# Two-layer gated expert network with a dense tower: order of the first transfers and of the first unit's products

## The reference

```python
e = jnp.stack([tbl_0[ids[:, 0]], ..., tbl_4[ids[:, 4]]], axis=1)     # 1024 rows x 5 tables x 1024
def _ple_layer(x, W, b, Gw, Gb, Gsw=None, Gsb=None):                 # 10 experts: 2 per task (4 tasks), 2 shared
    xe = x[:, EXPERT_IN_IDX, :]
    eo = jax.nn.relu(jnp.einsum('bed,edh->beh', xe, W) + b)          # each 1024 x 1024
    gates = jax.nn.softmax(jnp.einsum('btd,tdk->btk', x[:, :T, :], Gw) + Gb, axis=-1)
    task_out = jnp.einsum('btk,btkh->bth', gates, eo[:, SEL, :])
    if Gsw is None:
        return task_out
    gs = jax.nn.softmax(x[:, T, :] @ Gsw + Gsb, axis=-1)
    shared_out = jnp.einsum('be,beh->bh', gs, eo)
    return jnp.concatenate([task_out, shared_out[:, None, :]], axis=1)
z = _ple_layer(_ple_layer(e, W0, b0, G0w, G0b, Gs0w, Gs0b), W1, b1, G1w, G1b)
h = jnp.concatenate([z.reshape(1024, -1), dense_ctx], axis=1)
h = jnp.maximum(h @ W_top1 + b_top1, 0.0)
h = jnp.maximum(h @ W_top2 + b_top2, 0.0)
y = h @ W_top3
```

## Time and profile before

| | us |
|---|---|
| median of 3 runs | 1983.0 (1982.62 to 1983.07) |
| profiled execution, its own time | 1983.02 |
| its span | 1981.0 |
| TensorE busy | 1973.8 |
| VectorE busy | 1352.5 |
| ACT busy | 702.6 |
| GpSimd busy | 170.1 |

### The profile page before, as it was taken

How to read it: one execution, slowest core, us unless ns; L and a number is a source line. 1 busy time by engine, 2 the same in 40 slices (tenths; PEclk the granted TensorE clock), 3 DMA queues, 4 the chain that set the end, 5 groups by cost and what they waited for, 6 DMA issues and landing times.

```text
span 1981.0 us, 25278 instructions
## 1 busy us (share of the span) xinstructions
PE 1973.8 (100%) x8898; PEld 1612.3 (81%) x8898; DVE 1352.5 (68%) x1335; ACT 702.6 (35%) x934; POOL 170.1 (9%) x152
## 2 busy tenths in 40 slices
PE   9999999999999999999999999999999999999999
PEld 7878878888788888888878788788887888888887
DVE  6488988895256765667555888898943666556564
ACT  3333233333233233332434233323333333433333
POOL 5630000000030002122033000000000000000000
PEclk9999999999999999999999999999999999999999
DMA  7543434333253334344344434334332424333331
GB/s 228 171 156 109 131 95 130 128 96 100 85 164 96 117 96 149 106 147 121 96 144 135 133 94 130 103 116 136 96 100 76 124 92 127 97 116 96 117 96 43
DMA packets 69102, 232.24 MB, mean 117 GB/s; under 512 B 10037, under 2 KB 11325, under 8 KB 69033
## 3 DMA queue, kind: packets, MB, share of 16 engines
q1 hardware_dynamic: 60664, 210.30, 34.6%
q0 software_dynamic: 7488, 20.98, 3.3%
q10 hardware_dynamic: 880, 0.10, 0.0%
HBM read 230.27 MB, written 1.08 MB: 117 GB/s over the span
## 4 chain that ended last, share of the span: by engine, by line
PE 99%; DMA 0%; ACT 0%; issue 0%; POOL 0%
PE main L370 30%; PE main L371 29%; PE main L372 29%; PE top L371 3%; PE top L370 3%; PE top L372 3%; PE gps L423 1%; PE gps L435 1%; DMA eo_sh<-in_tbl,idx 0%; PE gps L410 0%; PE top L503 0%; DMA idx<-in_ids 0%; ACT eo_b L795 0%; PE top L561 0%; PE main L561 0%
## 5 line engine op out<-in xcount | busy, mean ns | idle before, releaser
L370 PE MATMUL main<-act_hi,w_hi 128*128 128x512 f32 (+1 forms) x2576 | 1002.0, 389 | 0.0
L371 PE MATMUL main<-act_lo,w_hi 128*128 128x512 f32 (+1 forms) x2576 | 1000.5, 388 | 0.0
L372 PE MATMUL main<-act_hi,w_lo 128*128 128x512 f32 (+1 forms) x2576 | 1000.5, 388 | 0.0
L932 DVE TENSOR_TENSOR w_lo<-raw,w_hi 128x1024 fp32r<-128x1024 f32 (+1 forms) x356 | 433.7, 1218 | 587.2 <-ACT w_hi L626 563.8
L626 ACT ACTIVATE w_hi<-raw 128x1024 fp32r<-128x1024 f32 (+1 forms) x356 | 376.4, 1057 | 1219.5 <-PE main L372 1109.1
L370 PEld LDWEIGHTS main<-act_hi,w_hi 128*128 128x128 f32 x2576 | 483.6, 188 | 107.6 <-issue 6.4
L372 PEld LDWEIGHTS main<-act_hi,w_lo 128*128 128x128 f32 x2576 | 483.6, 188 | 100.2
L371 PEld LDWEIGHTS main<-act_lo,w_hi 128*128 128x128 f32 x2576 | 483.6, 188 | 99.0
L1051 DVE TENSOR_TENSOR slots<-slots,prod 128x1024 f32<-128x1024 f32 (+2 forms) x202 | 245.0, 1213 | 6.0
L361 POOL DMA_INDIRECT slots<-in_tbl,idx x144 | 166.0, 1153 | 894.5 <-DVE act_lo L944 605.8
L1045 DVE TENSOR_TENSOR prod<-eo_sh,gate_b 128x1024 f32<-128x1024 f32 x136 | 165.7, 1219 | 1.7
(11 more groups left out here) (78 smaller groups left out, 419.9 us busy)
## 6 DMA issues: line engine op xcount, KB each, us to landing
raw<-in_w SPq DMA_DIRECT2D x304, 512.0 KB
gate_b<-tasks_dram SPq DMA_DIRECT2D x32, 512.0 KB, 5.9
raw<-in_w_top SPq DMA_DIRECT2D x32, 512.0 KB
raw<-in_w_first SPq DMA_DIRECT2D x16, 512.0 KB
gate_b<-tasks_dram SPq DMA_DIRECT2D x16, 256.0 KB, 6.4
slots<-in_tbl,idx POOLq DMA_INDIRECT x144
gate_b<-gates_dram SPq DMA_DIRECT2D x2, 512.0 KB, 4.0
raw<-in_w_top SPq DMA_DIRECT2D x4, 256.0 KB
```

The costliest lines, as they stand in the source:

```text
L370: nc.tensor.matmul(dst, lhs_hi, rhs_hi, start=start, stop=False)
L371: nc.tensor.matmul(dst, lhs_hi, rhs_lo, start=False, stop=False)
L372: return nc.tensor.matmul(dst, lhs_lo, rhs_hi, start=False, stop=stop)
L932: nc.vector.tensor_tensor(w_lo[0:parts, slot, 0:cols], raw[0:parts, rawslot, 0:cols], w_hi[0:parts, slot, 0:cols], ALU.subtract).then_inc( ...
```

## The change

SP issues weight unit 0 first of all. The row numbers of the first four tiles (4 columns, 2 KB, a semaphore `idx0_in` of their own), the identity, the other row numbers, and all constants as one tensor `fixed` (190 columns) are issued by ACT. Units 1 and 2 are issued behind row tiles 2 and 3, then the gate weights, then unit 3. The warming is 13 matrix products of a zero tile (`blank`, cleared by VectorE as its first instruction) instead of 18 transposes of the identity, and starts before the identity is there. The first unit's products of the first columns are taken apart: the high x high products (`x0_main`) of strips 0 to 3 stand behind tile 1, those of strips 4 to 7 inside tile 2, the others (`x0_cross`) around the rest of tile 2 and tile 3. The second columns are as before. The first bank of the turned strips is `main[1]` in place of `main[0]`.

```diff
-WARM = 18
+WARM = 13
+FIXED = (NE * KT, NE * KT, MT1, MT2, MT2, GBIAS)
...
-        bias0 = sb("bias0", [P, NE * KT])
-        bias1 = sb("bias1", [P, NE * KT])
-        tower_c = sb("tower_c", [P, MT1 + 2 * MT2])
+        fixed = sb("fixed", [P, sum(FIXED)])
+        cuts = np.cumsum((0, *FIXED)).tolist()
+        bias0, bias1, bias_t1, bias_t2, w3, gbias = (fixed[:, a:b] for a, b in zip(cuts, cuts[1:]))
...
-        x0_bank = [main[0], gps[1]] + top + [gps[0], main[1]]
+        x0_bank = [main[1], gps[1]] + top + [gps[0], main[1]]
+        blank = eo_b[:, 0, 0:P]
...
-            sp.dma_start(idx[:, :], ids).then_inc(idx_in, 16)
-            sp.dma_start(ident, ident_in).then_inc(ident_rdy, 16)
-            sp.dma_start(gw[:, :, :].rearrange("p k n -> p (k n)"), gs_first).then_inc(gw_in, 16)
...
-                    for c in range(RAW):
-                        if c:
-                            sp.wait_ge(x0_in[c], 16)
-                        unit(w0_first, c, c, c)
+                    unit(w0_first, 0, 0, 0)
+                    sp.wait_ge(x0_in[NBT - 2], 16)
+                    unit(w0_first, 1, 1, 1)
+                    sp.wait_ge(x0_in[NBT - 1], 16)
+                    unit(w0_first, 2, 2, 2)
+                    sp.dma_start(gw[:, :, :].rearrange("p k n -> p (k n)"), gs_first).then_inc(gw_in, 16)
+                    unit(w0_first, 3, 3, 3)
...
-            pool.wait_ge(idx_in, 16)
+            pool.wait_ge(idx0_in, 16)
...
+            pe.wait_ge(blank_rdy, 1)
+            for n in range(WARM):
+                nc.tensor.matmul(gps[0][:, 0:P], blank, blank, start=True, stop=True)
             pe.wait_ge(ident_rdy, 16)
-            for n in range(WARM):
-                nc.tensor.transpose(gps[0][:, 0:P], ident, ident)
...
+            def x0_main(ks):
+                for k in ks:
+                    pe.wait_ge(act_hi_rdy, k // 2 + 1)
+                    nc.tensor.matmul(main[0][:, 0:X0_COLS], w_hi[:, 0, k * P:(k + 1) * P], act_hi[:, k, 0:X0_COLS],
+                                     start=(k == 0), stop=False)
+            def x0_cross(ks):
+                for k in ks:
+                    pe.wait_ge(act_lo_rdy, k // 2 + 1)
+                    w = slice(k * P, (k + 1) * P)
+                    nc.tensor.matmul(main[0][:, 0:X0_COLS], w_hi[:, 0, w], act_lo[:, k, 0:X0_COLS], start=False, stop=False)
+                    nc.tensor.matmul(main[0][:, 0:X0_COLS], w_lo[:, 0, w], act_hi[:, k, 0:X0_COLS],
+                                     start=False, stop=(k == KT - 1))
...
-            for bt in range(X0_HALF + 1):
-                x0_turn(bt)
+            x0_turn(0)
+            x0_turn(1)
             pe.wait_ge(hi_split, 1)
+            x0_main(range(4))
+            x0_turn(2, range(6))
+            x0_main(range(4, KT))
             pe.wait_ge(lo_split, 1)
-            x0_sums(0, range(2))
-            x0_turn(X0_HALF + 1)
-            x0_sums(0, range(2, KT))
-            x0_sums(1, range(KT)).then_inc(unit_done, 1)
+            x0_cross(range(2))
+            x0_turn(2, range(6, KT))
+            x0_cross(range(2, 4))
+            x0_turn(3)
+            x0_cross(range(4, KT))
...
-            for dst, src in ((bias0, b0), (bias1, b1), (bias_t1, b_top1), (bias_t2, b_top2), (w3, w_top3)):
-                act.dma_start(dst[:, :], src).then_inc(consts_in, 16)
-            act.dma_start(gbias[:, :], g_bias).then_inc(consts_in, 16)
+            act.dma_start(idx[:, 0:NBT], ids[:, 0:NBT]).then_inc(idx0_in, 16)
+            act.dma_start(ident, ident_in).then_inc(ident_rdy, 16)
+            act.dma_start(idx[:, NBT:], ids[:, NBT:]).then_inc(idx_in, 16)
+            act.dma_start(fixed[:, :], fixed_in).then_inc(consts_in, 16)
...
+            nc.vector.memset(blank, 0.0).then_inc(blank_rdy, 1)
             nc.vector.memset(turned[:, :, :], 0.0).then_inc(chain, 1)
```

More of the change, by code:

```diff
@@ L61, with build @@
 Q4 = 4
-WARM = 18
+WARM = 13
 ROWSETS = 5 * NBT
 GBIAS = NE + (T // DUO + 1) * T
+FIXED = (NE * KT, NE * KT, MT1, MT2, MT2, GBIAS)
 IDX = NBT + (ROWSETS * HALVES - NBT) * Q4
 RAW = 4
-def build(nc, ids, dense, tbl_0, tbl_1, tbl_2, tbl_3, tbl_4, w0_first, w0, w1, w_top, w_top2, w_top3,
-          b0, b1, b_top1, b_top2, gs_first, gs_w, g_w, g_bias, ident_in, out):
+def build(nc, ids, dense, tbl_0, tbl_1, tbl_2, tbl_3, tbl_4, w0_first, w0, w1, w_top, w_top2,
+          gs_first, gs_w, g_w, fixed_in, ident_in, out):
     f32, f32r, i32 = mybir.dt.float32, mybir.dt.float32r, mybir.dt.int32
@@ L101, in build @@
         turned = sb("turned", [DUO * GCOL, N // GCOL, GCOL])
-        gbias = sb("gbias", [P, GBIAS])
-        gbias_tasks = gbias[:, NE + T // DUO * NG:]
         blocks = N // GCOL
@@ L114, in build @@
         idx = sb("idx", [P, IDX], i32)
-        bias0 = sb("bias0", [P, NE * KT])
-        bias1 = sb("bias1", [P, NE * KT])
-        tower_c = sb("tower_c", [P, MT1 + 2 * MT2])
-        bias_t1, bias_t2, w3 = tower_c[:, 0:MT1], tower_c[:, MT1:MT1 + MT2], tower_c[:, MT1 + MT2:]
+        fixed = sb("fixed", [P, sum(FIXED)])
+        cuts = np.cumsum((0, *FIXED)).tolist()
+        bias0, bias1, bias_t1, bias_t2, w3, gbias = (fixed[:, a:b] for a, b in zip(cuts, cuts[1:]))
+        gbias_tasks = gbias[:, NE + T // DUO * NG:]
         gates_dram = nc.dram_tensor("gates_dram", (HALVES, GROWS * N), f32, kind="Internal").ap()
@@ L129, in build @@
         idx_in = sem("idx_in")
+        idx0_in = sem("idx0_in")
+        blank_rdy = sem("blank_rdy")
         raw_in = [sem(f"raw_in{i}") for i in range(RAW)]
@@ L548, in tower3, with x0_turn @@
                 mm.then_inc(y_done, 1)
+            pe.wait_ge(blank_rdy, 1)
+            for n in range(WARM):
+                nc.tensor.matmul(gps[0][:, 0:P], blank, blank, start=True, stop=True)
             pe.wait_ge(ident_rdy, 16)
-            for n in range(WARM):
-                nc.tensor.transpose(gps[0][:, 0:P], ident, ident)
-            def x0_turn(bt):
+            def x0_turn(bt, ks=range(KT)):
                 pe.wait_ge(x0_in[bt], 16)
                 half, c = divmod(bt, X0_HALF)
-                for k in range(KT):
+                for k in ks:
                     at = (k % 2) * X0_COLS + c * P
@@ L564, in x0_turn @@
                         mm.then_inc(x0_turned, 1)
-            def x0_sums(half, ks):
-                n = slice(half * X0_COLS, (half + 1) * X0_COLS)
+            def x0_main(ks):
                 for k in ks:
-                    pe.wait_ge(act_hi_rdy, half * (KT // 2) + k // 2 + 1)
-                    pe.wait_ge(act_lo_rdy, half * (KT // 2) + k // 2 + 1)
-                    w = slice(k * P, (k + 1) * P)
-                    mm = three(main[0][:, n], w_hi[:, 0, w], w_lo[:, 0, w], act_hi[:, k, n], act_lo[:, k, n],
-                               k == 0, k == KT - 1)
-                return mm
@@ L585, in _ @@
+            x0_cross(range(4, KT))
+            rest = slice(X0_COLS, N)
+            for k in range(KT):
+                pe.wait_ge(act_hi_rdy, KT // 2 + k // 2 + 1)
+                pe.wait_ge(act_lo_rdy, KT // 2 + k // 2 + 1)
+                w = slice(k * P, (k + 1) * P)
+                mm = three(main[0][:, rest], w_hi[:, 0, w], w_lo[:, 0, w], act_hi[:, k, rest], act_lo[:, k, rest],
+                           k == 0, k == KT - 1)
+            mm.then_inc(unit_done, 1)
             expert(1, 1, 1)
@@ L836, in _ @@
             split_hi(1, 1, 0)
-            act.wait_ge(consts_in, 16 * 6)
+            act.wait_ge(consts_in, 16)
             for h in range(HALVES):
@@ L1238, in _ @@
             x0_again(range(0, 2))
-            dve.wait_ge(consts_in, 16 * 6)
+            dve.wait_ge(consts_in, 16)
             turns = ({"A": {3: [(0, 0, 0)], 4: [(0, 0, 1)], 5: [(0, 0, 2)], 7: [(0, 0, 3)],
@@ L1378 @@
             a["W_top2"].reshape(2, 2, P, TOP2).transpose(0, 2, 1, 3).reshape(2, P, 2 * TOP2)),
-        "w_top3": per_part(a["W_top3"]),
-        "b0": per_part(a["L0_rec_b0"][order]), "b1": per_part(a["L0_rec_b1"][order]),
-        "b_top1": per_part(a["b_top1"]), "b_top2": per_part(a["b_top2"]),
         "gs_first": quad_cols(a["L0_rec_Gs0w"]),
@@ L1385 @@
                          for some in (*(_quarters(a["L0_rec_G0w"])[t:t + DUO] for t in range(0, T, DUO)), a["L0_rec_G1w"])]),
-        "g_bias": np.concatenate([
+        "fixed_in": np.concatenate([
+            per_part(a["L0_rec_b0"][order]), per_part(a["L0_rec_b1"][order]), per_part(a["b_top1"]), per_part(a["b_top2"]),
+            per_part(a["W_top3"]),
             np.tile(a["L0_rec_Gs0b"].reshape(1, -1), (P, 1)),
```

## The result

The changed kernel takes 1985.97 us in the median of 22 runs (1984.77 to 1987.24), the kernel before 1983.49 in 22 runs beside it (1982.52 to 1984.03): 2.5 us slower, ratio 1.0013 with a 95% interval of 1.0007 to 1.0018. It lies within 0.2% of before, but outside my range, which ended at 1985.4. The profiled execution is near the top of these, 1987.1 us of its own time, with a span of 1985.0 against 1981.0; its rows show more of the loss than the median has.

A forecast was written before the change was run, and what follows sets the result against it. TensorE, saturated after 12.6 us, bounds the kernel, so only the head can move. Tile 1's landing +0.4 (0.8 - 0.4) and order +0.4 give +0.8 us on 1983.02, shaded to +0.6: 1983.6 us, range 1981.6 to 1985.4.

The forecast's parts named there:

- Step (a): Row numbers on ACT's queue beside weight unit 0: they land 0.8 us later, bounds 0 and +1.4.
- Step (e): Warming by 13 zero products: ends before tile 0, costs nothing itself; clock taken to rise where it did.
- Rival 2: TensorE's clock rises 3 us later after the earlier end of warming: +1.5 us, 1985.1 us; chance 0.18.
- (b): Row tiles no longer meet weight unit 0 in the DMA queues: 0.4 us given back, bounds 0 and 0.9.
- (c): Later weights issued behind the row tiles still land in time: cost 0, without that cover up to 1 us.
- (d): ACT issues 4 transfers for 6, so unit 0's split may start at about 4.5 us: effect 0.
- (f): New product order: gaps behind tile 1 and a wait for VectorE before the logits, +0.4 us, bounds 0 and +0.9.
- Rival 1: Row numbers pass ahead of the weights and rows arrive up to 0.9 us earlier: -0.6, 1982.4 us; chance 0.22.
- Rival 4: ACT's transfers always reach the engines later than SP's; row numbers land with weight unit 0: +1.4, 1984.8 us; chance 0.09.
- the gather at 3.7 to 4.1 us: Sign for the row numbers' delay: GpSimd's first gather starts then instead of at 3.12 us.
- tile 1 at 10.4 to 11.0: Sign for the rows' landing: row tile 1 is there at 10.4 to 11.0 us.
- the turns of tile 0 at 0.23: Sign for the warming: turns of tile 0 and most of tile 1 spaced 0.23 us on TensorE.

The follow-up runs named there:

- e2: Changed kernel with 28 warming products instead of 13; 1984.69 us.
- e9: Kernel before with weight unit 0 first on SP, then identity and gate weights, and row numbers first on ACT; 1985.15 us.
- e1: Changed kernel with the first tiles' row numbers issued by SP ahead of weight unit 0; 1982.90 us.
- e5: Changed kernel with SP issuing weight unit 0 only once the row numbers on ACT's queue have landed; 1983.52 us.
- e7: Kernel before with 22 warming transposes instead of 18; 1983.06 us.
- e4: Changed kernel with row numbers on SP ahead of weight unit 0 and 20 warming products; 1982.57 us.
- e6: Kernel before with only the new warming, 13 products of a zero tile; 1983.04 us.
- e3: Changed kernel with the old order of the first unit's products and the old first bank; 1985.70 us.
- e10: e4 with units 1 to 3 issued behind row tiles 1 to 3 and gate weights behind unit 0, as before; 1982.84 us.
- e8: e4 with the old order of the first unit's products and the old first bank; 1982.87 us.
- e12: e4 repeated without change; 1982.76 us.

## Why the prediction was wrong

The bound was read rightly: nothing moved but the head, the logits' start moved by 3.93 us and the span by 4.0. The forecast's form (tile 1 later, less what the rows win) was right too, and the time still left its range, by two steps. The first alone would not have done it: e2, with the row numbers as late and the clock steady, has 1984.69 us, below the 1985.4 where the range ended.

**Step (a), mis-sized.** I put the row numbers' delay at +0.8 us, with +1.4 as the bound. It is +1.97 (4.81 against 2.84), and in e9 +1.7. The mechanism, packets taking turns with those of the weights, is what the queues show. The size failed in three terms. The row numbers' packets took 1.90 us from the first to the last start (2.34 to 4.24), not the 1.4 of 9 turns at 0.16, and 0.71 in the kernel before (1.75 to 2.46), so +1.2 for +0.8. The first of them started 0.6 us later than before, which I had put at nothing, and from the last to the landing it took 0.2 longer. The weight unit before was a guide at hand: issued at 2.13, split from 6.05, 3.9 us; "lands with the weights" meant at 0.75 + 3.9 = 4.65, so a bound of +1.8. The Trainium skill's sentence on round-robin by packets ("DMA: Bandwidth & Descriptors", Queues, rings and completion order) agrees with e1, e5 and e9 together in the direction; but by that page an engine drains a whole packet of typically 9 to 17 descriptors before it switches, which would be all of the 9 that it has of the weight unit, while here 70 of the row numbers' 128 pieces had started by 3.4 us. So they took turns in smaller portions. I had placed its result in my bounds, and should have taken it for the estimate.

**Step (e), "in the sum it rises where it did".** This was false. By the mean clock (0.998 or 0.999) in all 22 runs of the changed kernel it was low for a time after it had risen, for about 7 us in the profiled one. Rival 2 had the direction and the size (+1.5; e2 gives 1.3 in the median, and the profiled run ends unit 0 2.27 us later behind tile 1 than the one of before) but the wrong picture: not a rise that comes later, but a rise during the warming (28 products in e2 take 8.26 us, 0.29 each; the first 13 take 0.35 each) and a fall behind 3.95 us of idle time, the turns of tile 0 and 1.27 more. The fall is made by (a) and (e) together: warming ends at 5.6 instead of 7.3 us while tile 0 comes at 9.5 instead of 8.3. Shortening the pause from either side cures it: e1 (pause 1.70) in 8 of 11 runs, e2 (0.19) in all. That idle time is behind the fall is shown by this; how much of it is too much is not: 1.85 us let the clock stand in all runs of e7, 1.75 in 3 of 11 of e5, and e9 with 0.47 and then 1.50 in 7 of 11. I also took the one profiled run of before for the kernel's habit; e7 shows that such transposes raise the clock within 4 us.

**The sum by measured terms.** Row numbers late: e2 less e4, 1984.69 - 1982.57 = 2.1 us. Clock: changed less e2, 1.3. All else, e4 less before: -0.75. Together +2.65, measured +2.5. The terms add up by construction, but for the two medians of before (1983.32 and 1983.49), and the split depends on the order: with the row numbers put right first they are worth 3.1 (changed less e1) and the longer warming 0.3 (e1 less e4), since early tiles also shorten the pause.

**The rest, point by point.**
- (b) forecast 0.4 us given back: from the first gather to tile 1 it was 7.24 us (10.36 - 3.12) and is 6.78 (11.86 - 5.08). Right, and not by one draw alone: with the transfers of before it is 7.2 to 7.6 (before, e6, e7), with those of the change 6.6 to 7.0 (changed, e2, e3).
- (c) no cost, no gain: right as far as e10 tells. TensorE never waited for unit 1.
- (d) right: the split starts at 4.64, forecast 4.5, and nothing waited for it.
- (f) forecast +0.4. The wait before the logits is there but tiny: in the changed kernel VectorE's rebuilding of x0 ends at 26.36 + 2.36 = 28.72 us, the last product before them starts at 28.51 and takes 0.23, and they start at 28.83. It did take VectorE's slack of 0.6 us, as forecast. What I missed is the gain on the other side, tile 2's landing, which the old order meets with a wait of 0.63 us in e8 and 0.31 in e7 once the clock is high. The net is nothing against e8 and +0.3 against e7, and the medians of e4, e12 and e8 show no cost: the forecast's size is met in one profile of the two, and not in the times.

```profile
26.36 2.36 DVE L1231 TENSOR_TENSOR slots<-act_hi,act_lo 128x1024 f32<-128x1024 f32 x2
```

- Rival 1 (numbers pass ahead of the weights) needs SP's queue, as in e1 and e4; in the change it did not happen. Rival 4 (ACT's queue slow) is refuted by e5, though what it foresaw, a landing with the weight unit, came by the other cause.
- Of what I had named as signs, the gather at 3.7 to 4.1 us (it came at 5.08), tile 1 at 10.4 to 11.0 (11.86) and the turns of tile 0 at 0.23 (0.11) all came out wrong, those of tile 1 at 0.21 only because the clock had fallen, the first product between tiles 1 and 2 right. The gap before the logits is 0.1 us.

## What to carry to other kernels

The transfer that starts a chain of landings, here 2 KB that every gather waits for, belongs ahead of the big one in the same queue, not beside it in another: beside, it landed here when the big one did. A warming should last until the real work arrives: in e2, e4, e8, e10 and e12, where it did to within 0.2 us in the profile, all 55 runs have a clock of 1.000; with pauses from 0.47 to 2.79 us it went either way, and a change that makes the work later also makes the pause longer. And a head of a few microseconds varies from run to run by its clock, so one profile of it is one draw: look at the granted clock of all runs before you put a level into a sum.

## What was not expected of the hardware

- A 2 KB transfer of 128 rows landed 1.59 us after its issue with no other queue's data beside it (e5), 1.94 and 1.98 ahead of a 512 KB one on the same queue (e4, e1), and 3.81 to 4.06 beside it on another queue (e9, changed).
- The granted clock fell after TensorE had taken up work again (tile 0 from 9.57 to 10.64, the fall at about 10.8, before tile 1), and stayed at 0.50 for some 7 us, 5.8 of them with TensorE busy without a pause.
- With a pause between warming and tile 0 (as profiled) of 1.70 us the clock stood in 8 of 11 runs (e1), of 1.75 in 3 of 11 (e5), of 1.85 in 11 of 11 (e7), of 3.95 in none of 22.
- Plain f32 products of a zero tile raise the clock as f32 transposes of an identity do (e2, e7).

What stays open: whether the new order gains 0.1 to 0.3 us, and whether e4 beats the kernel before beyond doubt; both are below what 11 runs tell. Open too is what decides between a clock that falls and one that stands at a pause of some 0.5 to 3 us; no experiment varied the pause alone over this range.
